# The Mlp turns of a fused graph kernel in a new order: second product one turn behind, transposes one ahead

## The reference

```python
xn = layernorm(x)
h  = relu(xn @ gnn_W1 + b1) @ gnn_W2 + b2
gnn = h + segment_sum(h[dst], src)                 # 100000 edges
k, q, v = split(layernorm(xn) @ kqv_w + kqv_b)     # the mix: an attention without softmax
y  = v + (attention(k, q, v, w) @ proj_w + proj_b)
mix = y + gelu(layernorm(y) @ mlp_w1 + b1) @ mlp_w2 + b2
x  = x + gnn + mix
out = haar_inverse(ffn(haar_forward(layernorm(x))))  # last part, per row
```

## Time and profile before

| | us |
|---|---|
| median of 3 runs | 1768.52 |
| lowest and highest run | 1767.4, 1773.77 |
| profiled execution, span from first to last instruction | 1853.0 |
| TensorE busy in it | 1586.3 |
| VectorE busy | 1135.8 |
| ScalarE busy | 827.2 |
| GpSimd busy | 998.1 |

### The profile page before, as it was taken

The page is one execution under the profiler, slowest core; times in us unless marked ns, Lnnn a source line. Parts: engine busy times, 40 slices in busy tenths (PEclk is TensorE's granted clock), DMA queues, the critical chain, the costliest instruction groups (busy, mean ns, idle before and its releaser), DMA issues.

```text
span 1853.0 us, 26852 instructions
## 1 busy us (share of the span) xinstructions
PE 1586.3 (86%) x8883; PEld 1264.3 (68%) x8883; DVE 1135.8 (61%) x2523; ACT 827.2 (45%) x1896; POOL 998.1 (54%) x1057
## 2 busy tenths in 40 slices
PE   5999999889588899998999967888888887689896
PEld 4778878777467677766677745777676766466664
DVE  6899998984234456444554444555555554377786
ACT  2144445444354434334444354555555554245552
POOL 3024434335556556665666666676666666455520
PEclk9999999999789899999999988999999999799998
DMA  6023332223235455555555564555555554556652
GB/s 184 21 75 115 90 97 84 84 89 106 80 100 164 142 150 160 166 158 154 156 156 159 158 191 149 164 174 171 174 168 176 170 176 145 154 176 202 205 168 76
DMA packets 88684, 263.65 MB, mean 142 GB/s; under 512 B 18556, under 2 KB 20604, under 8 KB 88547
## 3 DMA queue, kind: packets, MB, share of 16 engines
q1 hardware_dynamic: 47490, 149.05, 24.1%
q0 software_dynamic: 41056, 112.88, 21.9%
HBM read 210.64 MB, written 44.90 MB: 138 GB/s over the span
## 4 chain that ended last, share of the span: by engine, by line
PE 42%; DVE 17%; issue 16%; ACT 8%; DMA 7%; another core or an unknown queue 6%; POOL 2%; SPq 1%; DVEq 1%; POOLq 0%; ACTq 0%
DVE sb_weights L1546 6%; PE bank L1007 4%; ACT sb_weights L1357 3%; DMA sb_step<-y_rows 3%; PE bank L973 2%; PE bank L975 2%; PE bank L974 2%; DMA sb_step<-sb_acc 2%; PE turn_bank L935 2%; PE bank L935 2%; DVE sb_step L1727 2%; PE bank L778 1%; PE bank L776 1%; PE bank L777 1%
## 5 line engine op out<-in xcount | busy, mean ns | idle before, releaser
L671 POOL DMA_INDIRECT sb_weights<-hidden_rows,sb_weights x830 | 824.7, 994 | 477.6 <-issue 209.7
L1357 ACT ACTIVATE sb_weights<-sb_const,sb_weights 128x125 f16<-128x125 f16 x880 | 266.5, 388 | 95.0 <-PE turn_bank L937 56.8
L1853 DVE TENSOR_TENSOR sb_acc<-sb_acc,turn_bank 125x257 f32 x220 | 92.5, 421 | 221.5 <-PE turn_bank L937 80.5
L1853 DVE TENSOR_TENSOR sb_acc<-sb_acc,bank 125x257 f32 x220 | 92.4, 420 | 206.3 <-remote 66.3
L1546 DVE TENSOR_TENSOR sb_weights<-sb_weights 128x512 f32<-128x512 f32 (+3 forms) x256 | 164.4, 684 | 3.6
L1275 ACT ACTIVATE sb_step<-sb_step 125x256 f32<-125x256 f32 x100 | 50.4, 507 | 251.4 <-DVE sb_step L1719 243.7
L776 PE MATMUL bank<-sb_w_parts,sb_x_high 128*125 128x512 f32 (+1 forms) x400 | 139.1, 348 | 0.0
L638 POOL TENSOR_SCALAR sb_const<-sb_const 125x2 f32<-125x2 f32 x25 | 10.2, 408 | 238.4 <-ACT sb_step L1259 238.4
L778 PE MATMUL bank<-sb_w_parts,sb_x_low 128*125 128x512 f32 (+1 forms) x400 | 135.2, 338 | 0.1
L777 PE MATMUL bank<-sb_w_parts,sb_x_high 128*125 128x512 f32 (+1 forms) x400 | 135.0, 337 | 0.0
L1361 ACT ACTIVATE sb_weights<-sb_weights,sb_const 128x1000 f16<-128x1000 f16 x110 | 124.2, 1129 | 3.6
(11 more groups left out here) (364 smaller groups left out, 4323.7 us busy)
## 6 DMA issues: line engine op xcount, KB each, us to landing
sb_step<-x SPq DMA_DIRECT2D x63, 500.0 KB
sb_step<-x_t SPq DMA_DIRECT2D x50, 500.0 KB
sb_weights<-hidden_rows,sb_weights POOLq DMA_INDIRECT x830
y_rows<-sb_step SPq DMA_DIRECT2D x25, 500.0 KB
sb_step<-y_rows SPq DMA_DIRECT2D x25, 500.0 KB
z_rows<-sb_step SPq DMA_DIRECT2D x25, 500.0 KB
sb_step<-z_rows SPq DMA_DIRECT2D x13, 504.0 KB
out<-sb_step SPq DMA_DIRECT2D x13, 500.0 KB
```

Of the source, the lines that this page charges most:

```text
L671: pool.indirect_dma_start(out=ring[:, r % RING * 2 + h, 0:HID], out_offset=None, in_=table, in_offset=bass.IndirectOffsetOnAxis(ap=row_of[ ...
L1357: mm = act.activation(hit[q % 2][:, i, :], iota_h[:, :], ACT.Abs, bias=less_lane[:, q * BP + i // 2, i % 2:i % 2 + 1])
L1853: dve.tensor_tensor(dst, dst, (BE, BH)[n % 2][0:P, 0:RW], ALU.add).then_inc(g_add, 1)
```

## The change

The Mlp stage gets another order. In turn `a` TensorE does the first half of the features of `a`, the transposes of `a+1`, the second product of `a-1` and then the second half of the features of `a`. Gelus, splits and `z_rows` follow suit: the second half of the gelus of `a-1` comes at the start of turn `a`, `z_rows(a-1)` at its end. The last second product moves into the join. The gelus of a half get a wait for the second product of the turn before (`m_mm`, now counted per half). There are three x buffers, the third in a place that the last stage uses for z; SP loads y first, then x when the z store of two turns before has landed, then stores z. Four of the eight groups of `BETWEEN` go into turn 0. The first transposes, their copies and their low halves move into the last attention step. `tail_weights` moves from turn 2 to turn 0 and its copy by ScalarE to turn 1; on ScalarE the copy of the high half of `mlp2_w` comes behind the first gelus; the late roots move from turn 1 to 2 and the late scales from 2 to 4. The sums of the last stage's first two steps are fetched ahead of turn 24's transfers, those of the second into the place of an odd y buffer.

```diff
-TURN, SECOND, BETWEEN, MLP, JOIN = (6, 14, 16), [14, 10, 9, 8] + [7] * (STEPS - 4), 8, [6] * STEPS, 6
+TURN, SECOND, BETWEEN, MLP, JOIN = (6, 14, 16), [14, 10, 9, 8] + [7] * (STEPS - 4), 4, [10] + [6] * (STEPS - 1), 6
...
-        z3 = x3
+        z3 = [x3[:, 0], x3[:, 1], z_first[2]]
...
             def late_io(a):
-                if a > 0:
-                    store_z(steps[a - 1])
-                if 0 < a and a + 1 < STEPS:
-                    z_stored(steps[a - 1])
-                    load_xd(steps[a + 1].j, steps[a + 1].s)
                 if a + 2 < STEPS:
                     sp.wait_ge(zadd, a + 2)
                     sp.wait_ge(h_rows, a + 2)
                     load_yd(steps[a + 2].j, steps[a + 2].s)
+                if 2 <= a and a + 1 < STEPS:
+                    z_stored(steps[a - 2])
+                    load_xd(a + 1)
+                if a > 0:
+                    store_z(steps[a - 1])
...
             sp.wait_ge(v_mm, STEPS + 1)
+            load_yd(0, 1)
+            load_xd(0)
             sp.dma_start(mlp2_w, chunks(d["L0_mix_mlp_w2"])).then_inc(w2m_in, 16)
-            load_xd(0, 0)
-            load_yd(0, 1)
-            load_xd(0, 1)
+            load_xd(1)
+            load_xd(2)
             store_y(Step(2, STEPS - 1))
...
             for a in range(STEPS):
+                if a == STEPS - 1:
+                    fetch_sums(steps[0])
+                    fetch_sums(steps[1])
                 late_io(a)
-            fetch_sums(steps[0])
             store_z(steps[STEPS - 1])
-            fetch_sums(steps[1])
...
                 pe.wait_ge(qtc, t.u + 2)
+                if last:
+                    pe.wait_ge(sq, 4 * STEPS + 1)
+                    transposes(each_step(0)[0])
...
-            transposes(steps[0])
             groups(BETWEEN)
-            pe.wait_ge(y_read, 2 * STEPS + 1)
             for a in range(STEPS):
                 counts = spread(MLP[a], 4)
                 features(steps[a], 0)
                 groups(counts[0])
-                features(steps[a], 1)
-                groups(counts[1])
                 if a + 1 < STEPS:
                     transposes(steps[a + 1])
                 else:
                     acc_transposes(steps[0])
-                pe.wait_ge(z_ok, a + 1)
                 if a == 0:
-                    pe.wait_ge(*made("mlp2_split"))
-                if a == 2:
+                    pe.wait_ge(y_read, 2 * STEPS + 1)
+                else:
+                    if a == 1:
+                        pe.wait_ge(*made("mlp2_split"))
+                        pe.wait_ge(ev("a_fc1"), 1)
+                    pe.wait_ge(z_ok, a)
+                    mlp2(steps[a - 1], 0)
+                groups(counts[1])
+                if a > 0:
+                    mlp2(steps[a - 1], 1)
+                groups(counts[2])
+                features(steps[a], 1)
+                groups(counts[3])
+                if a == 0:
                     tail_weights()
-                mlp2(steps[a], 0)
-                groups(counts[2])
-                mlp2(steps[a], 1)
-                groups(counts[3])
+            joint = spread(JOIN, 3)
             pe.wait_ge(late_in, 5 * 16 + 1)
             pe.wait_ge(ev("w2_scaled"), 1)
             w2_products(steps[0])
+            pe.wait_ge(z_ok, STEPS)
+            mlp2(steps[STEPS - 1], 0)
             acc_transposes(steps[1])
-            groups(JOIN // 2)
+            groups(joint[0])
+            mlp2(steps[STEPS - 1], 1)
+            groups(joint[1])
             degree_transposes(steps[0])
             w2_products(steps[1])
+            groups(joint[2])
             x1_closed(steps[0])
...
                 act.wait_ge(feat, t.g * 2 + i + 2)
+                act.wait_ge(m_mm, max(1, t.u * 2 + i))
...
                 if a + 1 < STEPS:
                     norm_rows(steps[a + 1])
-                act.wait_ge(m_mm, a + 1)
-                gelus(steps[a], 0)
+                if a > 0:
+                    gelus(steps[a - 1], 1)
...
                 hits_until(ahead)
-                gelus(steps[a], 1)
                 if a + 1 < STEPS:
                     copy_hT(steps[a + 1])
                 else:
                     copy_accT(steps[0])
-                hits_until(ahead + sum(counts[0:2 if a == 2 else 3]))
+                gelus(steps[a], 0)
...
+                hits_until(ahead + sum(counts[0:2]))
...
+                if last:
+                    hT_low(each_step(0)[0])
+                    add_groups(BETWEEN)
                 row_stats(y_out[0:P, t.s], t, own2).then_inc(y_ok[t.s], 1)
...
-                if a == 2:
+                if a == 4:
                     scales(EARLY, NT, "other_roots", "other_scales")
                 elif a == 3:
                     late_weights()
+                if a > 0:
+                    split_gelus(steps[a - 1], 1)
+                add_groups(counts[0])
                 skip_rows(steps[a])
-                add_groups(counts[0])
-                if a == 0:
-                    split_mlp2()
-                split_gelus(steps[a], 0)
-                add_groups(counts[1])
-                split_gelus(steps[a], 1)
                 if a + 1 < STEPS:
                     hT_low(steps[a + 1])
                 else:
                     sums_low(steps[0])
+                add_groups(counts[1])
+                split_gelus(steps[a], 0)
+                if a == 0:
+                    split_mlp2()
                 add_groups(counts[2])
-                z_rows(steps[a])
+                if a > 0:
+                    z_rows(steps[a - 1])
                 add_groups(counts[3])
```

More of the change, by code:

```diff
@@ L384, in build_program @@
             "r_weights_in", "norm_weights_in", "k_weights_in", "k_rows_in", "q_weights_in", "v_weights_in", "slot_numbers_in"))
-        x_ld, x2_ld, xt_ld, x3_ld, y_ld = (pair(n) for n in ("x_in", "x2_in", "xT_in", "x3_in", "y_in"))
+        x_ld, x2_ld, xt_ld, y_ld = (pair(n) for n in ("x_in", "x2_in", "xT_in", "y_in"))
+        x3_ld, z_st = ([sem(f"{n}{k}") for k in range(3)] for n in ("x3_in", "z_stored"))
         acc_ld = pair("sums_in")
-        r_st, y_st, z_st = (pair(n) for n in ("r_stored", "y_stored", "z_stored"))
+        r_st, y_st = (pair(n) for n in ("r_stored", "y_stored"))
         z_ld, o_st = ([sem(f"{n}{k}") for k in range(7)] for n in ("z_in", "out_stored"))
@@ L516, in fetch_sums @@
                 elif t.u == 1:
-                    sp.wait_ge(m_mm, STEPS + 1)
+                    sp.wait_ge(zadd, STEPS)
+                    sp.wait_ge(h_rows, STEPS)
                 else:
@@ L520, in fetch_sums @@
                     sp.wait_ge(deg_tr, t.u)
+                    if t.u == 3:
+                        sp.wait_ge(m_mm, 2 * STEPS + 1)
                 sp.wait_ge(g_add, pairs_of_smallest(t.u) + 1)
@@ L963, in mlp1_columns, with transposes @@
                 mm.then_inc(made("mlp1_columns")[0], 1)
+            def transposes(t):
+                pe.wait_ge(h_rows, t.g + 2)
+                pe.wait_ge(h_t, t.g * 2 + 1)
+                for bk, cs in ((BF, (0, 1)), (BG, (2, 3))):
+                    for i, c in enumerate(cs):
+                        for m in (0, 1):
+                            last = pe.transpose(bk[:, i * 250 + m * P:i * 250 + m * P + P],
+                                                h3[0:P, m, c * 128:(c + 1) * 128], ident[0:P, 0:P])
+                    last.then_inc(tr, 1)
             def phase2(t, last):
@@ L1043, in _ @@
                 phase2(t, t.u == STEPS - 1)
-            def transposes(t):
-                pe.wait_ge(h_rows, t.g + 2)
-                pe.wait_ge(h_t, t.g * 2 + 1)
-                for bk, cs in ((BF, (0, 1)), (BG, (2, 3))):
-                    for i, c in enumerate(cs):
-                        for m in (0, 1):
-                            last = pe.transpose(bk[:, i * 250 + m * P:i * 250 + m * P + P],
-                                                h3[0:P, m, c * 128:(c + 1) * 128], ident[0:P, 0:P])
-                    last.then_inc(tr, 1)
             def features(t, i):
@@ L1180, in _ @@
             steps = each_step(0)
-            pe.wait_ge(qtc, STEPS + 1)
-            pe.wait_ge(sq, 4 * STEPS + 1)
+            groups(BETWEEN)
             pe.wait_ge(w_ok, 4 * STEPS + 1)
             pe.wait_ge(*made("mlp1_split"))
-            transposes(steps[0])
-            groups(BETWEEN)
-            pe.wait_ge(y_read, 2 * STEPS + 1)
             for a in range(STEPS):
@@ L1952, in mlp1_halves, with hT_low @@
                 dve.drain().then_inc(made("mlp1_split")[0], 1)
+            def hT_low(t):
+                for i, bk in ((0, BF), (1, BG)):
+                    part = lambda h: hT3[:, t.s, h, 2 * i:2 * i + 2, :].rearrange("p a b -> p (a b)")
+                    dve.wait_ge(hT_high, t.g * 2 + i + 2)
+                    dve.tensor_tensor(part(1), bk[:, 0:500], part(0), ALU.subtract).then_inc(h_t, 1)
             def phase2(t, more, last):
@@ L2002, in _ @@
                 phase2(t, t.u < STEPS - 2, t.u == STEPS - 1)
```

(7 more changed lines are left out.)

58 lines of the change are left out of this document (32 added, 26 removed).

## The result

| kernel | median us | lowest to highest |
|---|---|---|
| before, six runs beside after | 1769.26 | 1763.9 to 1774.38 |
| after | 1754.35 | 1751.36 to 1760.7 |

The ratio is 0.9914, interval 0.9895 to 0.9932: 15 us faster, where 52 were forecast, and outside the range (1682 to 1750). The profiled execution of after has a span of 1750.1 us at 1752.63 us.

A forecast was written before the change was run, and what follows sets the result against it. Two loops bound the turn: the DMA round, and gelu, split, second product; afterwards the row-transfer queue. Start 19 + turns 39 - join 5 = 53 us: 1853.0 becomes 1800, or 1717 at the timed median; range 1682 to 1750.

The forecast's parts named there:

- Turn order: Mlp turns: no work added; TensorE has work over gelus and splits, covering the 2.3 us gap seen before.
- The turn after: Mlp turn of the changed kernel: 16.5 us, bound by queue q1 serving three row transfers of 5.5 us each.
- q1's share: Sign of being right: the row-transfer queue's share near 5/16 of the DMA engines almost throughout.
- ScalarE's wait for y: Sign of being right: this wait in the Mlp turns, 65.1 us in the profile, nearly gone.
- The loop that the prediction set aside: Mlp turns: y and x loads, then skip rows, 14.4 us if z does not come between; below 16.5.
- The turn before: Mlp turn of the unchanged kernel: 18.2 us, so 1.7 us gained a turn, 39 us over 23 turns.
- The start: From the first transposes to turn 1: turn 1 begins at 1117 instead of 1136.16, 19 us sooner.
- the wait of the tail weights for their constants: Turn 0: the product, moved there, waits for its constants until about 1114, plus 2.8 us.
- the start gives its lower bound: Rival, chance 0.10: constants and y queue in one burst; start gains 5 us instead of 19, time 1731.
- The join: Turn 24 to the last stage: last z store 27 us into the turn instead of 22, a loss of 5 us.
- Faster queue: Rival, chance 0.20: GpSimd and its ring bind the Mlp turn at 15.8 us; gain 69 us, time 1699.
- No effect: Rival, chance 0.07: turn stays near 18.2 us, only the start gains, 14 us or less; time 1755 to 1768.

The follow-up runs named there:

- e9: After with the gathers of the Mlp turns left out, so its sums are wrong: 1762.54 us, ratio to before 0.9472.
- e10: After, unchanged, timed and traced in a short execution: 1756.25 us, ratio to before 0.9922.
- e4: After, unchanged, timed and traced in a long execution: 1839.34 us, ratio to before 1.0002.
- b_fifth: Before, unchanged, run once for its trace in a short execution: 1773.81 us.
- b_third: Before, unchanged, run once for its trace in a long execution: 1847.27 us.
- e11: After with the gathers of the turns bringing 256 bytes of each row instead of 1024, so its sums are wrong: 1712.06 us, ratio to before 0.9671.
- e8: Before with the gathers of the Mlp turns left out, so its sums are wrong: 1785.24 us, ratio to before 0.9582.
- e1: After with the tail weights product moved back to turn 2 and ScalarE's copy of it to turn 3: 1845.39 us, ratio to before 1.0009.
- e7: After with the first sums tile's transposes, copy and low half moved behind turn 24's second features half: 1862.31 us, ratio to before 1.0008.
- e13: After with the tail weights product at the end of turn 2 and turn 2's y load ahead of the constants: 1753.53 us, ratio to before 0.9901.
- e14: e13 with the edit of e7 added: 1744.77 us, ratio to before 0.9838.

## Why the prediction was wrong

**Turn order: mechanism right.** TensorE's gaps behind the splits are gone, no work was added, and e9 shows the order free of any wait of its own. TensorE busy 91% at clock 0.99 (forecast: above 90%, near 1.0).

**The turn after: right, for the kind that was timed.** Forecast 16.5 from three transfers of 5.5, measured 16.40 in the first trace of after and 16.47 in e10, with landings 5.48 us apart and q1 empty for 0.34 us a turn: the queue is the bound, as said. Two signs did not come. q1's share was 23.9% and not five sixteenths, since beside the gathers its packets are under way on 3.8 of its five engines in the mean; and ScalarE's wait for y stayed, since in a full queue y is used 8.4 to 10.4 us after its issue. The loop that the prediction set aside, 14.4 us "if z does not come between", is the place: z did come between. That no release came late was luck: in the long kind, from which the forecast was read, the turn after is 17.90 (e4).

**The turn before: wrong, 14 us.** The term that failed is the 18.2 us of a turn before. 18.2 us came from z stores 0 to 23 of a long execution. It holds the long turns 1 and 2 and the extra time of such an execution; from turn 3 on it is 18.07 in that trace and 17.51 in a short one. I took the 84.5 us between trace and median off evenly, after the sum; but they lie where the gathers run. Both kinds run alike, to about 2 us, until 446 us; the first copy of VectorE behind TensorE's product of line 1025, where the gathers have just begun, starts at 470.01 in b_fifth and at 477.49 in b_third, and the distance grows from there (turn 0 begins at 1039.45 and 1103.21). A gain worked out from waits of the long kind was credited to the short: there before loses 1.83 us a turn to an empty queue, and the change wins 1.0, not 1.7.

**The start: wrong, 20 us, the largest miss.** The term that failed is the wait of the tail weights for their constants. "Until about 1114, plus 2.8. Turn 1 then begins at 1117, 19 us sooner." The tail weights product started not about 17 us after the first features but 38.3 (1033.46 to 1071.81). I gave no number to the step that decides: SP's four constants. In e10 their issue alone lasts from 1039.83 to 1061.50, and y of turn 2 stands behind them:

```profile
1039.83 3.06 SPq L577 DMA_DIRECT2D sb_weights<-L_gnn_W  x1
1042.94 0.47 SPq L579 DMA_DIRECT2D sb_step<-fc_t  x1
1043.45 10.15 SPq L580 DMA_DIRECT2D sb_weights<-c_interp  x1
1053.65 7.85 SPq L581 DMA_DIRECT2D sb_weights<-fc_t  x1
1061.62 2.38 SPq L491 DMA_DIRECT2D sb_step<-y_rows  x1
```

The stretch that I meant to shorten was also 16.5 us shorter in a short execution to begin with: from the first transposes to turn 1 it takes 48.5 us in the long trace and 32.0 in b_fifth. The rival "the start gives its lower bound" had the right place, but its bound of +5 was no bound: turn 1 alone lost 16.4, and up to turn 3 the gain was 2.1.

**The join: sign right, 4 us more.** Last z store forecast 27 us behind the start of turn 24, measured 39.6, since the sums' transposes, moved into turn 24, wait 10.70 us for their fetch; but from that store to the product only 11.3 us pass, not 18.4. A slip beside it: 1577.41 - 1554.76 is 22.6 and not 22, 0.6 us of the loss.

**The rivals.** "Faster queue" is what e9 and e11 show when the gathers or their bytes are away; with them the queue is neither fast nor slow (5.4 us of work a transfer). "No effect" is what e4 shows for long executions.

## What to carry to other kernels

When a consumer of constants is moved ahead, write down when its data lands: every transfer on that queue ahead of it, with the issue time that the profile shows for it; if the stretch is a burst, changing the order only changes who waits. Before a sum is made from waits in a trace, check that the trace is of the kind of execution that is timed; if its span is 5% longer, find where the excess lies before scaling it away. A loop that runs through a queue should be priced as what the queue serves in a turn, with the transfers' times beside the other traffic, plus the time in which it stands empty: a reordering can win back only the second, here at most 1.8 us a turn.

## What the hardware showed that I had not expected

In long executions engines are released late where gathers run. After in a long execution (e4): TensorE ends line 1047 at 469.62, VectorE waits for just that and starts 9.0 us later.

```profile
468.93 0.69 PE L1047 MATMUL bank<-sb_const 1*128 1x256 f32 x2
```

```profile
478.65 1.29 DVE L1910 COPY sb_step<-bank 128x512 f32<-128x512 f32 x2 [23.32 <-remote]
```

In the first trace of after (short) the same copy starts as TensorE ends:

```profile
468.66 1.29 DVE L1910 COPY sb_step<-bank 128x512 f32<-128x512 f32 x2 [14.34 <-PE bank L1047]
```

Up to there VectorE's instructions are within 1.1 us of each other in the two executions. From TensorE's counts in the trace of e4, 173 of 219 between 1110 and 1440 us are recorded over 1 us behind the end of the matmul that makes them (some records are missing; by the records alone it is 144 of 195); in the first trace of after none of 240 is. From 20 to 440 us, ahead of the gathers, none of 151 is late in e4. In e8 and e9, long executions too, it is 4 of 233 and 5 of 274 in the turns, where no gathers run. So late counts go with the gathers, but only in some executions. It is not the chip: the one that took 1861.96 for before beside e7 to e9 took 1771.9 beside e13 and e14. All 68 timed runs of before beside e1 to e9 are long (1835 to 1865 us) and all 34 beside the others short (1764 to 1777), so the kind held through a whole series of runs; only the first trace of before is long while the three runs timed with it are short. What sets it stays open.
